# A mixture-of-experts layer behind attention: tokens get their slots in ranges by expert during attention, through indirect transfers, and queries and keys are turned later in a step

## What is computed

```python
router_logits = jnp.einsum('td,de->te', x_flat, moe_router)
topk_logits, topk_idx = jax.lax.top_k(router_logits, TOP_K)
topk_weights = jax.nn.softmax(topk_logits, axis=-1).astype(x.dtype)
...
sort_idx = jnp.argsort(expert_ids, axis=0)
...
w13_out = jax.lax.ragged_dot(x_sort, moe_w13, group_sizes)
gate, up = jnp.split(w13_out, [MOE_DIM], axis=-1)
hidden = jax.nn.silu(gate) * up
out_dispatch = jax.lax.ragged_dot(hidden, moe_w2, group_sizes)
out_flat = jnp.zeros_like(x_flat).at[token_ids_sort].add(out_dispatch * w_sort[:, None], mode='drop')
```

## Time and profile before

| | |
|---|---|
| time, median of 3 runs | 871.74 us (870.18 to 874.94) |
| time of the profiled execution | 879.68 us |
| its span | 877.9 us |
| instructions | 27588 |
| PE busy | 742.9 us (85%) |
| DVE busy | 565.2 us (64%) |
| ACT busy | 396.6 us (45%) |
| POOL busy | 438.8 us (50%) |
| mean granted TensorE clock, share of full speed | 0.904 |

### The profile page before, as it was taken

How to read it: one execution, slowest core, us unless ns; L and a number is a source line. 1 busy time by engine, 2 the same in 40 slices (tenths; PEclk the granted TensorE clock), 3 DMA queues, 4 the chain that set the end, 5 groups by cost and what they waited for, 6 DMA issues and landing times. The chain is left out here.

```text
span 877.9 us, 27588 instructions
## 1 busy us (share of the span) xinstructions
PE 742.9 (85%) x9892; PEld 518.6 (59%) x9892; DVE 565.2 (64%) x1164; ACT 396.6 (45%) x881; POOL 438.8 (50%) x612
## 2 busy tenths in 40 slices
PE   4957999899998999888911189999999999999994
PEld 3734667666766776666700156665666666666662
DVE  6756989777886787776269735555555555555552
ACT  0223666577777776876410033333333333333331
POOL 5662454455555565443223535555555555455552
PEclk9885999998998999998555589999999999999998
DMA  6577566454554554543210013333333333333332
GB/s 238 167 233 232 163 201 200 125 152 141 154 155 139 169 155 138 153 123 111 61 25 1 6 38 56 62 52 60 56 56 62 62 56 57 61 56 58 60 61 25
DMA packets 64856, 91.80 MB, mean 105 GB/s; under 512 B 13160, under 2 KB 45688, under 8 KB 64663
## 3 DMA queue, kind: packets, MB, share of 16 engines
q1 hardware_dynamic: 49655, 66.81, 25.2%
q0 software_dynamic: 15072, 23.21, 15.4%
HBM read 58.95 MB, written 24.10 MB: 95 GB/s over the span
## 5 line engine op out<-in xcount | busy, mean ns | idle before, releaser
L1240 POOL DMA_INDIRECT out<-y,token_of x76 | 120.5, 1586 | 141.4 <-DMA out<-y,token_of 107.5
L1285 DVE SCALAR_TENSOR_TENSOR hid<-quad,up_scale,silu 128x512 f32<-128x512 f32 x76 | 57.0, 751 | 100.3 <-PE quad L1321 99.1
L1321 PE MATMUL quad<-w_hi,x_hi 128*128 x304 | 116.2, 382 | 1.1 <-DVE x_lo L1292 1.1
L514 DVE TENSOR_REDUCE nm_src<-quad 69x16 f32<-69x1104 f32 x64 | 83.3, 1302 | 52.1 <-PE quad L825 51.7
L1321 PE MATMUL quad<-w_lo,x_hi 128*128 x304 | 116.1, 382 | 0.0
L1321 PE MATMUL quad<-w_hi,x_lo 128*128 x304 | 116.0, 382 | 0.0
L705 ACT ACTIVATE probs<-quad 69x1104 f32<-69x1104 f32 x64 | 69.7, 1089 | 59.2 <-PE quad L893 58.5
L1233 POOL DMA_INDIRECT xg<-xn_rows,token_of x76 | 75.4, 993 | 35.5 <-issue 19.5
L1253 ACT ACTIVATE hid_hi<-bank 128x512 f16<-128x512 f32 x76 | 45.4, 597 | 104.3 <-PE bank L1340 104.3
L1265 ACT ACTIVATE x_hi<-bank 128x256 f16<-128x256 f32 x76 | 29.1, 383 | 123.5 <-PE bank L1361 123.5
L1321 PE MATMUL bank<-w_hi,hid_hi 128*128 x304 | 82.9, 273 | 1.6 <-ACT hid_hi L1253 1.6
(11 more groups left out here) (213 smaller groups left out, 1888.2 us busy)
## 6 DMA issues: line engine op xcount, KB each, us to landing
w_lo<-in_experts_w SPq DMA_DIRECT2D x24, 512.0 KB, 5.9
w_raw<-in_experts_w SPq DMA_DIRECT2D x48, 256.0 KB, 4.8
xt<-in_patches SPq DMA_DIRECT2D x18, 384.0 KB, 5.7
h<-h_rows SPq DMA_DIRECT2D x34, 128.0 KB, 5.5
hb<-h_rows SPq DMA_DIRECT2D x34, 128.0 KB
out<-h SPq DMA_DIRECT2D x34, 128.0 KB, 4.2
xn_rows<-xn SPq DMA_DIRECT2D x34, 128.0 KB, 4.4
vb<-v SPq DMA_DIRECT2D x30, 138.0 KB
```

The costliest lines, as they stand in the source:

```text
L514: nc.vector.tensor_reduce(nm_src[b % 2][:, :].rearrange("p (g j) -> p g j", g=4)[:, :, 0:4], quad[0:SEQ, :, 0:4 * SEQ].rearrange("p g (j k ...
L1240: nc.gpsimd.indirect_dma_start(out, bass.IndirectOffsetOnAxis(token_of[:, n:n + 1], 0), y[q][:, :], None, compute_op=ALU.add).then_inc(add ...
L1285: nc.vector.scalar_tensor_tensor(out=hid[q][:, :], in0=quad[:, 2 * q + 1, :], scalar=up_scale[:, :], in1=silu[q][:, :], op0=ALU.mult, op1= ...
L1321: last = nc.tensor.matmul(dst, x[:, k, :], w[:, bass.ds(col + k * (2 * width if width == HIDDEN else width), width)], start=(k == 0 and m ...
```

## The change

In `routing`, the picking, counting and placing go. In their place:

- Tiles come in five blocks (8, 8, 8, 8 and 3). When the logits of a block's last tile are there, DVE picks in the next two steps (PICK1, PICK2), PE counts at PLACE what stands ahead of each token for each expert, and DVE adds the start of the expert's range and makes the slot numbers. An expert's range is fixed: 35 tiles.
- From the step behind that, POOL writes (token number, weight) to the slot by indirect transfers, one per tile and choice, 70 in all, each of up to 128 rows of 32 bytes, into a table in DRAM (`slots`), which one transfer fills with spare numbers at step 4. For blocks 0 to 2 that is one tile a step, in steps 25 to 32, 40 to 47 and 55 to 62. The tiles of block 3 go at steps 70 to 75, three of them at 75 with the three of block 4. Before DVE fills `sent` for a block, it waits until all the earlier blocks' transfers have landed.
- `routing` is left with eleven small operations on DVE, one gather of the 76 rows in use (4 KB each), and two turns that give `token_of` and `weight_of`.
- `front` has four steps more (up to 75). `xn_rows` has 256 columns, and `experts` lacks L1307 and L1312.

In the steps, the turn of queries and keys comes behind PE's scores and its other turns; the row load HL comes behind the stores on SP; values are loaded one step later, into a ring of 4; a patch tile's `zout` comes at the end of ACT's step; six patch tiles, not seven, come before step 0, and twelve between attention steps, each of them one step nearer to its need; the texts go in three pieces: 12 elements at the start, 24 at step 1, 28 at step 9.

```diff
-V_RING, VB_RING = 3, 5
+V_RING, VB_RING = 3, 4
-TXT_FIRST = 8
-LAST_STEP = BATCH + 8
+TXT_PARTS = [0, 12, 36, 64]
+TXT_STEP = [None, 1, 9]
+BLOCK = 8
+BLOCKS = [(lo, min(lo + BLOCK, G)) for lo in range(0, G, BLOCK)]
+SLOT = 8
+EXPERT_TILES = G
+TABLE_PARTS, TABLE_TILES = 96, 3
+LAST_STEP = BATCH + 12
+ATTENTION_END = BATCH + 8
-EARLY = [-10, -9, -8, -7, -6, -5, -4]
+EARLY = [-10, -9, -8, -7, -6, -5]
...
                 BT, ST4, XN2, LG = ({back[g] + k: g for g in range(G)} for k in range(4))
+                PICK1, PICK2, PLACE = ({back[hi - 1] + 3 + k: i for i, (lo, hi) in enumerate(BLOCKS)} for k in range(1, 4))
+                SEND = {}
+                for i, (lo, hi) in enumerate(BLOCKS):
+                    for g in range(lo, hi):
+                        SEND.setdefault(min(back[hi - 1] + 7 + g - lo, LAST_STEP - 1), []).append(g)
+                mm_step, latest = EARLY + [0] * (NT - EARLIEST), ATTENTION_END
                 for n in reversed(range(EARLIEST, NT)):
-                    k = min(first[need[n]] - 10, latest - 3)
+                    k = min(first[need[n]] - 9, latest - 3)
...
-                            b = t + 1
+                            b = t
                             if 0 <= b < BATCH:
...
+                            for g in SEND.get(t, ()):
+                                pool.wait_ge(s["slots_ready"], g // BLOCK + 1)
+                                if g == 0:
+                                    pool.wait_ge(slots_blank, 16)
+                                    pool.wait_ge(s["slot_consts"], 5)
+                                for j in range(TOP_K):
+                                    nc.gpsimd.indirect_dma_start(slots, bass.IndirectOffsetOnAxis(slot_i[0:rows[g], j, g:g + 1], 0),
+                                                                 sent[0:rows[g], j, g % BLOCK, :], None).then_inc(placed, 16)
+                            for i in range(1, 3):
+                                if t == TXT_STEP[i]:
+                                    lo, hi = TXT_PARTS[i:i + 2]
+                                    pool.dma_start(by_batch[lo:hi, 1 + PATCHES:, :], txt[lo:hi, :, :]).then_inc(txt_in[i], 16)
...
+
+                        def choose(j, k, from_):
+                            each_expert = [P, k, EXPERTS]
+                            order = rev[:, None, :].broadcast_to(each_expert)
+                            pick_then(nc.vector.tensor_reduce(top[:, j, 0:k], from_, AX.X, ALU.max))
+                            pick_then(nc.vector.tensor_tensor(hit[:, 0:k, :], from_, top[:, j, 0:k, None].broadcast_to(each_expert), ALU.is_equal))
+                            pick_then(nc.vector.tensor_tensor(hit[:, 0:k, :], hit[:, 0:k, :], order, ALU.mult))
+                            pick_then(nc.vector.tensor_reduce(hit_max[:, 0:k], hit[:, 0:k, :], AX.X, ALU.max))
+                            pick_then(nc.vector.tensor_tensor(pick[:, j, 0:k, :], order, hit_max[:, 0:k, None].broadcast_to(each_expert), ALU.is_equal))
...
+                        def read_places(i):
+                            lo, hi = BLOCKS[i]
+                            k = hi - lo
+                            dve.wait_ge(s["place_mm"], i + 1)
+                            nc.vector.tensor_tensor(place[:, 0:k, :], quad[:, 3, 4 * SEQ:4 * SEQ + k * EXPERTS].rearrange("p (k e) -> p k e", e=EXPERTS),
+                                                    base[:, None, :].broadcast_to([P, k, EXPERTS]), ALU.add).then_inc(s["place_ready"], 1)
+
+                        def slots_of(i):
+                            lo, hi = BLOCKS[i]
+                            k = hi - lo
+                            dve.wait_ge(s["place_ready"], i + 1)
+                            for j in range(TOP_K):
+                                pick_then(nc.vector.tensor_tensor(own[:, j, 0:k, :], pick[:, j, 0:k, :], place[:, 0:k, :], ALU.mult))
+                            for j in range(TOP_K):
+                                pick_then(nc.vector.tensor_reduce(slot_f[:, j, 0:k], own[:, j, 0:k, :], AX.X, ALU.add))
+                            pick_then(nc.vector.tensor_copy(slot_i[:, :, lo:hi], slot_f[:, :, 0:k]))
+                            dve.wait_ge(s["gap_exp"], i + 1)
+                            pick_then(nc.vector.tensor_scalar(hit_max[:, 0:k], gap[:, 0:k], 1.0, None, ALU.add))
+                            pick_then(nc.vector.reciprocal(gate[:, 0, 0:k], hit_max[:, 0:k]))
+                            pick_then(nc.vector.tensor_tensor(gate[:, 1, 0:k], gate[:, 0, 0:k], gap[:, 0:k], ALU.mult))
+                            if lo:
+                                dve.wait_ge(placed, 16 * TOP_K * lo)
+                            pick_then(nc.vector.tensor_copy(sent[:, :, 0:k, 0], ids[:, None, lo:hi].broadcast_to([P, TOP_K, k])))
+                            nc.vector.tensor_copy(sent[:, :, 0:k, 1], gate[:, :, 0:k]).then_inc(s["slots_ready"], 1)
+                            pick_then(nc.vector.tensor_reduce(block_sum[:, :], both[:, 0:k, :].rearrange("p k e -> p e k"), AX.X, ALU.add))
+                            pick_then(nc.vector.tensor_tensor(total[:, :], total[:, :], block_sum[:, :], ALU.add))
 
                         def qkv_scale():
...
+                            if t in PLACE:
+                                read_places(PLACE[t])
...
+                            if t in PLACE:
+                                slots_of(PLACE[t])
+                            if t in PICK2:
+                                second_choice(PICK2[t])
+                            if t in PICK1:
+                                first_choice(PICK1[t])
...
+                        def find_places(i):
+                            lo, hi = BLOCKS[i]
+                            k = hi - lo
+                            pe.wait_ge(s["both_ready"], i + 1)
+                            pe.wait_ge(s["halves_set"], 3)
+                            at = quad[:, 3, 4 * SEQ:4 * SEQ + k * EXPERTS]
+                            nc.tensor.matmul(at, prefix_h[:, :], both[:, 0:k, :].rearrange("p k e -> p (k e)"), start=True, stop=False)
+                            for m in range(k - 1):
+                                behind = quad[:, 3, 4 * SEQ + (m + 1) * EXPERTS:4 * SEQ + k * EXPERTS].rearrange("p (k e) -> p k e", e=EXPERTS)
+                                nc.tensor.matmul(behind, ones_h[:, :], both[:, m, None, :].broadcast_to([P, k - 1 - m, EXPERTS]), start=False, stop=False)
+                            nc.tensor.matmul(at.rearrange("p (k e) -> p k e", e=EXPERTS), ones_h[:, :], total[:, None, :].broadcast_to([P, k, EXPERTS]),
+                                             start=False, stop=True).then_inc(s["place_mm"], 1)
...
-                            if t == QKV_STEP:
-                            if t in QT:
-                                g = QT[t]
...
+                                find_places(PLACE[t])
                             b = t
...
+                            if t in QT:
+                                g = QT[t]
+                                r = rows[g]
...
+                        pool.wait_ge(placed, 16 * TOP_K * G)
+                        pool.wait_ge(row_ready, 1)
+                        nc.gpsimd.indirect_dma_start(found[:, :, :].rearrange("t l c -> t (l c)"), None, slots.rearrange("(t l) c -> t (l c)", l=P),
+                                                     bass.IndirectOffsetOnAxis(row_i[0:TILES_MOE, 0:1], 0)).then_inc(found_in, 16)
```

More of the change, by code:

```diff
@@ L181, in front @@
                 START = mm_step[0] - 2
-                assert mm_step[EARLIEST] > 2 and all(mm_step[n] <= first[need[n]] - 10 for n in range(NT))
+                assert mm_step[EARLIEST] > 2 and all(mm_step[n] <= first[need[n]] - 9 for n in range(NT))
                 XL = {mm_step[n] - (2 if n < EARLIEST else 5): n for n in range(2, NT)}
@@ L189, in front @@
                 PEAK_STEP = SCALE_STEP + 1
-                QKV_STEP = START + 2
-                assert 0 <= PEAK_STEP < CHUNK_FROM
+                QKV_STEP = START + 3
+                assert 0 <= PEAK_STEP < CHUNK_FROM and PEAK_STEP not in PLACE
+                assert all(t < BATCH or t >= BATCH + 3 for t in PLACE)
                 def tile_of(token):
@@ new lines, in second_choice @@
+                        def second_choice(i):
+                            lo, hi = BLOCKS[i]
+                            k = hi - lo
+                            choose(1, k, less[:, 0:k, :])
+                            nc.vector.tensor_tensor(gap[:, 0:k], top[:, 1, 0:k], top[:, 0, 0:k], ALU.subtract).then_inc(s["gap_ready"], 1)
+                            if hi == G:
+                                pick_then(nc.vector.memset(pick[rows[G - 1]:, :, k - 1, :], 0.0))
+                            nc.vector.tensor_tensor(both[:, 0:k, :], pick[:, 0, 0:k, :], pick[:, 1, 0:k, :], ALU.add).then_inc(s["both_ready"], 1)
@@ L1169, in _ @@
```

(10 more changed lines are left out.)

380 lines of the change are left out of this document (149 added, 231 removed).

## The result

The changed kernel takes **907.9 us** (median of 4 runs, 904.6 to 909.5), the kernel before 872.7 (4 runs, 870.2 to 874.9). The ratio is 1.038, with an interval of 1.033 to 1.043: slower by 35 us where 17 us less were forecast. The profiled execution took 904.6 us with a span of 902.8, 24.9 more than the span before.

The account below looks back on a forecast made before the run. PE and its hand-overs with DVE were taken to pace attention, with 56 us of `routing` exposed. Terms -16 -8 +3 -8 +6 +6 +1 -1 sum to -17: 871.7 to 855 us; forecast's range 845 to 867, whole range 840 to 880.

Parts of the forecast that it names:

- Writes on POOL in attention, +6: Attention: 48 writes in 24 steps, two a step, just fit POOL's time; a quarter us a step, ends 0 and 21.
- The late turn, -8: Attention: PE no longer waits 6.3 us for POOL's qk, and perhaps 2 us of its wait for maxima go.
- Row load and values "at zero": Attention: the reordered row load and values loaded a step later cost nothing, since both have steps of slack.
- Routing, -16: Behind the last logits: 56 us go, a shorter chain set by POOL comes; first gather at 486.5, where it was 502.46.
- Picks, +6: Attention: DVE's picks for three blocks, 26 operations each, show as 2 us a block; ends 0 and 18.
- Patch tile, +3 and -3: The seventh patch tile adds 3 us to attention and takes 3 us off the stage before step 0.
- `experts`, -1: Start of `experts`: the gather need not wait for L1307; -1 us, ends -8 and 3.
- Before step 0, -8: First stage: moving texts saves 5 of DVE's 7.15 us wait for the row load; one patch tile less saves 3.
- "POOL the bound": Rival, 0.12: a write above 1.45 us makes 24 attention steps run at POOL's pace; 883 us.
- "The writes wait for DVE": Rival, 0.06: DVE holds POOL up, each of the 48 writes in attention loses 0.74 us; 877 us.
- Those of being wrong: A write above 1.45 us, POOL over 90% busy in steps 25 to 32, or PE waiting longer for maxima during picks.
- signs of being right: 22 writes of 1.0 to 1.3 us, one 2 us gap, first gather some 37 us behind logits, attention about 8 longer.

Follow-up runs that it names:

- stand-ins: Changed kernel with each of the 48 writes in attention replaced by a plain POOL addition of 352 columns and a wait for its end: 878.8 us, 1.006.
- few rows: Changed kernel with the 48 writes in attention sending 16 rows each instead of 128: 882.5 us, 1.010.
- the order alone: Kernel before with the new order of steps, texts in three pieces and six early patch tiles, but the old routing: 874.8 us, 1.002.
- texts alone: Kernel before with the texts in three pieces (12, 24 and 28 elements) and nothing else: 873.7 us, 1.000.
- the early turn: Changed kernel with only the early turn of queries and keys put back: 894.7 us, 1.023.

## Why the prediction was wrong

The shape of the sum held; one term of it was wrong by more than all the others together.

- **Writes on POOL in attention, +6: the step that failed.** It measures 44 us in the runs, 40 of them in attention. The price of a write (1.033 us and 0.30) was right, and so was what POOL does in a step: busy for 4.4 us, where 5.25 with the gaps stood in the sum. The conclusion, that "it just fits" and costs a quarter us a step, was not: the steps grew from 5.6 to 6.8 us, POOL was busy for 65% of them, and PE was stopped. The term asked only whether POOL has the time. POOL's late results alone cost 15 us (stand-ins), where 6 were given. The other 29 come with the transfer: 25 with the rows sent, and 4 as a longer end of the block. The 25 are seen on PE: as pauses, and as a granted clock of 0.90, where it is 0.93 with few rows and 0.94 without writes. The upper end of 21 was a bound for POOL's time alone, so the range left them out.
- **The late turn, -8:** -5.6 where nothing is sent, which is near it, and +13 beside the writes. The two parts of the change were costed apart and are not independent.
- **Row load and values "at zero":** 6 us without slots (874.8 against 869.1, with `zout`); beside the writes the row load is worth 2, within what can be measured. The text named DVE's wait for h as the sign, and it came: 24.9 us with the order alone. "Steps of slack" was a count of steps, not a look at what stands ahead of the load on SP, where stores wait for POOL's zout and values for PE.
- **Routing, -16:** -8.8. The writes went as forecast: 22 of them with one gap of 1.9 us, 29.1 us from the first start to the last end, 30.6 forecast. The block's end was taken from a block without writes, 0.3 for 7.0, and the gather from one of 128 rows of 1 KB, 2.7 us short: the rows moved for 4.0 us, mostly at 105 GB/s, where 216 GB/s stood in the sum. Of the 7.0 us at the block's end, 4 are those of the 48 earlier writes above. The Trainium skill's price for a DMA (DMA: Bandwidth & Descriptors, Anatomy of one DMA), by which the gather was estimated at 2.7 us, does not hold for it: 6.3 were measured, in the run without writes too.
- **Picks, +6:** 5.4, right, and seen as PE's wait of 6.1 us for them. **Patch tile, +3 and -3:** 3.8 and 4.1 in the profiles, right. **`experts`, -1:** nothing. **Before step 0, -8:** 14.1 in the profile, but with texts alone the runs show no gain. The 7.15 us of DVE's wait came from the one profile of the kernel before, which was above its median.
- **The rivals.** "POOL the bound" needed writes above 1.45 us; they take 1.03. "The writes wait for DVE" gave 877. By the Trainium skill (SBUF — State Buffer, Who interferes with whom), DVE would hold up POOL's descriptors; the longest write in attention is 1.72 us and the mean 1.07 against 0.96 behind it, so some 5 us in 48 writes can be of this kind. With the early turn it is 8 (mean 1.14): three writes take over 2 us, up to 2.45, and each of them began under DVE's maximum with DVE's split of weights (L662) right behind. (Half of the excess of 2.12 over 0.57 is 0.78, not 0.74, which moves this rival by 1 us.) Both rivals looked for the cost in POOL, as the forecast did; no case had it in PE.
- **The signs.** Those of being wrong stayed away, though the forecast was wrong: the writes in attention took 1.07 us on the mean (5 of 48 took 1.3 to 1.72), POOL was busy for 69% of steps 25 to 32, and PE waited less for maxima (8.1 us in attention, 13.4 before). All of them looked at POOL and DVE. Of the signs of being right, the 22 writes (0.96 us each) and their gap came, and two failed: attention became 46.9 us longer rather than 8, and the first gather of `experts` followed the last logits by as many, 46.9 us, rather than 37.

What stays open: why PE pauses beside a pair of writes with the late turn and hardly with the early one. The pauses come with writes of all their rows (42 against 15 with few rows) and with the late turn (42 against 8), they stand under POOL's instruction and just behind it rather than under the packets, and no semaphore explains them. Open too is how much of what the writes cost with the early turn is the lower clock and how much is POOL's late qk.

## What to carry to other kernels

A free slot on a side engine prices only its own time. Before small scattered writes are put under a stage that PE bounds, replace them once by plain operations of the same length and once by the same writes with few rows: the two differences tell what the engine costs and what the transfer costs. And cost parts of a change together where they meet in the same step; here one part was worth 6 us alone and cost 13 beside the other.

## What was not expected of the hardware

- Indirect writes of 128 rows of 32 bytes slow an engine that has no part in them: a series of 32 matmuls takes 1.68 us beside one, where it takes 0.69 undisturbed, and 0.69 to 0.71 beside such a write in another order.
- A write of 16 rows takes POOL 0.85 us and one of 128 rows 0.96 when nothing else runs: the rows hardly matter to the instruction, and much to the rest.
- The end of a block waits about 0.1 us for each indirect write issued in it (0.5, 3.1 and 7.0 us for 0, 22 and 70), long after most had landed: DVE waits for the landing of 64 of the 70 before it fills the last block's `sent`.
- An indirect gather of 76 rows of 4 KB lands 6.3 us behind its start: 1.9 until the first row moves, then 4.0, mostly at 105 GB/s.
